# A macaron block on one core: the up product multiplied on GpSimd, the first FFN an item ahead, ten steps for eleven

## What is computed

```python
x = x + 0.5 * ffn(layernorm(x))
x = x + mamba_and_mlp(layernorm(x))
x = x + 0.5 * ffn(layernorm(x))        # the same ffn weights

def ffn(x):                             # mixture of 32 experts of 96, six chosen, and a shared part of 192
    scores = sigmoid(x @ gate_w); combine = top 6 of them, normalised
    act = silu(x @ wg) * (x @ wu)
    return (combine * act) @ wd + (silu(x @ sg) * (x @ su)) @ sd

def mamba_and_mlp(x):
    h = x + mamba(rmsnorm(x))           # projections, conv, softplus, a scan over 256 tokens with 16 states, gate, out
    return h + mlp(rmsnorm(h))          # silu(gate) * up, down, 1024 wide
```

## Time and profile before

| | |
|---|---|
| median of 3 runs | 1908.88 us (1899.79 to 1910.92) |
| the profiled execution | 1911.02 us, its span 1909.2 us |
| mean granted TensorE clock | 0.936 |
| step -1, ends at | 20.7 us |
| step 0 | 93.5 us, to 114.2 |
| step 1 | 180.0 us, to 294.2 |
| step 2 | 200.0 us, to 494.2 |
| step 3, 4, 5, 6 | 217.8, 218.5, 218.4, 218.5 us, to 1367.4 |
| step 7 | 201.9 us, to 1569.3 |
| step 8 | 187.4 us, to 1756.7 |
| step 9 | 85.3 us, to 1842.0 |
| step 10 and the end | 67.2 us, to 1909.2 |

### The profile page before, as it was taken

How to read it: one execution, slowest core, us unless ns; L and a number is a source line. 1 busy time by engine, 2 the same in 40 slices (tenths; PEclk the granted TensorE clock), 3 DMA queues, 4 the chain that set the end, 5 groups by cost and what they waited for, 6 DMA issues and landing times. The chain is left out here.

```text
span 1909.2 us, 25234 instructions
## 1 busy us (share of the span) xinstructions
PE 1600.1 (84%) x7512; PEld 1197.6 (63%) x7512; DVE 1318.9 (69%) x2331; ACT 703.8 (37%) x1418; POOL 724.8 (38%) x838
## 2 busy tenths in 40 slices
PE   6776778667889888889889898888989998677999
PEld 5665557556765557555665557555666566556998
DVE  3236984689468964899468874799559974896343
ACT  4234424533343423534344333534344324532211
POOL 4511552245225532355225532355225632353222
PEclk9887889888899999999999999999999999988999
DMA  7852223323232222322232222222232222323563
GB/s 256 300 165 95 83 93 92 115 83 106 69 107 85 82 79 79 106 75 88 81 101 89 71 85 87 96 79 88 84 97 94 82 90 69 125 94 103 176 211 132
DMA packets 72751, 204.77 MB, mean 107 GB/s; under 512 B 12928, under 2 KB 22368, under 8 KB 72224
## 3 DMA queue, kind: packets, MB, share of 16 engines
q1 hardware_dynamic: 64416, 177.86, 27.9%
q0 software_dynamic: 8192, 25.17, 4.5%
HBM read 179.39 MB, written 15.73 MB: 102 GB/s over the span
## 5 line engine op out<-in xcount | busy, mean ns | idle before, releaser
L610 PE MATMUL gub<-x_hi,wr 128*128 128x256 f32 (+1 forms) x1144 | 454.9, 398 | 76.6 <-DVE hid L978 55.2
L690 PE MATMUL acc<-hid,w_down 128*128 128x256 f32 (+1 forms) x1144 | 419.4, 494 | 0.8 <-DVE hid L978 0.8
L1236 POOL TENSOR_TENSOR hid<-hid,weight 128x256 f32<-128x256 f32 (+1 forms) x264 | 266.6, 1010 | 384.0 <-DVE hid L978 366.6
L612 PE MATMUL gub<-x_hi,wr 128*128 128x256 f32 (+1 forms) x1144 | 394.5, 345 | 0.0
L611 PE MATMUL gub<-x_lo,wr 128*128 128x256 f32 (+1 forms) x1144 | 394.4, 345 | 0.0
L839 ACT ACTIVATE hid<-gub 128x256 f32<-128x256 f32 (+1 forms) x350 | 160.8, 460 | 619.3 <-PE gub L612 530.7
L1249 POOL TENSOR_TENSOR ring<-ring 128x512 f32<-128x512 f32 x192 | 246.7, 1285 | 318.6 <-DVE ring L1133 318.6
L1127 DVE TENSOR_TENSOR_SCAN ring<-decays,side 128x512 f32<-128x512 f32 x256 | 310.2, 1212 | 10.7 <-ACT decays L936 8.3
L610 PEld LDWEIGHTS gub<-x_hi,wr 128*128 128x128 f32 x1144 | 230.1, 201 | 114.3 <-issue 67.9
L690 PEld LDWEIGHTS acc<-hid,w_down 128*128 128x128 f32 x1144 | 212.2, 201 | 86.2 <-issue 67.2
L612 PEld LDWEIGHTS gub<-x_hi,wr 128*128 128x128 f32 x1144 | 229.5, 201 | 23.1
(11 more groups left out here) (115 smaller groups left out, 1691.2 us busy)
## 6 DMA issues: line engine op xcount, KB each, us to landing
wr<-w_halves SPq DMA_DIRECT2D x260, 512.0 KB, 3.3
wm_gu<-in_w_mlp POOLq DMA_DIRECT2D x64, 256.0 KB, 3.0
w_halves<-wr SPq DMA_DIRECT2D x26, 512.0 KB, 4.8
wm_down<-in_w_mlp POOLq DMA_DIRECT2D x64, 128.0 KB, 2.5
w_raw<-in_w_gu SPq DMA_DIRECT2D x26, 256.0 KB, 4.9
cst<-decays SPq DMA_DIRECT2D x192, 32.0 KB, 1.9
...
```

Of the source, the lines that this page charges most:

```text
L610: mm(out, w[:, 0, half, k, :], x_hi[:, k, a:b], start=(k == 0), stop=False)
L612: last = mm(out, w[:, 1, half, k, :], x_hi[:, k, a:b], start=False, stop=(k == KC - 1))
L690: last = mm(acc[k][:, a:b], w, h[:, a:b], start=(c == 0), stop=(c == (MLP_CHUNKS if mlp else FFN_CHUNKS) - 1))
L1236: nc.gpsimd.tensor_tensor(h, h, weight[c // 3 % CSLOTS][:, a:b], ALU.mult).then_inc(sem["weighted"], 1)
```

## The change

Two edits. First, item `u` gets a part on ScalarE, which copies the bank to one of three new SBUF buffers `u_sb` and so frees the bank; `by_u` moves from DVE to POOL, which multiplies `hid` by that buffer, and the subtraction in `ws` moves from POOL to DVE. The MLP's products stay on DVE under a semaphore of their own, `m_hidden`.

Second, the first FFN runs an item ahead. Step 0 has item 0 alone, and norms and routes items 1 and 2. Step 1 takes items 1 and 2 in one 512-wide pass (`twin`); step t from 2 to 6 takes item t+1. The result is kept in `x1_next` and copied over to `x1` by a DMA (`shift`) once mamba has done with that, and the raw x of the next item is then loaded to `x1_next` (`again_n`). The second FFN takes item t-3 in steps 3 to 7 as before; from step 7 on it also takes the item whose MLP ran in the same step (`own`: item 5 in step 7, 6 in step 8, 7 in step 9), in columns 0 to 255. In these steps the MLP, norm `ln2a` and routing are merged with mamba's norms and projections, and the whole FFN pass comes after, merged with the scan. The steps are -1 to 9, the loop has three turns (3, 4, 5). The widths are 256 in steps 0, 2, 8, 9 and 512 in 1 and 3 to 7.

The core of the diff:

```diff
 def items_of(t):
-    first, mamba, mlp, second = (0 <= t - lag < BATCH for lag in range(4))
-    following = t + 1 < BATCH
     if t < 0:
-        return [("load",)] + norm("ln1") + routing("f1")
-    hand = ([("hx", "f1")] if first else []) + ([("hx", "f2")] if second else [])
-    hand += ([("rt2", "f1")] if first else []) + ([("rt2", "f2")] if second else [])
+        return [("load", 0)] + norm("ln1") + routing("f1")
+    mamba, mlp = 0 <= t - 1 < BATCH, 0 <= t - 2 < BATCH
+    first, twin, second, own = t < BATCH - 1, t == 1, 3 <= t < BATCH, t >= BATCH - 1
+    ready = (["f1"] if first else []) + (["f2"] if twin or second else [])
+    hand = [("hx", call) for call in ready] + [("rt2", call) for call in ready]
+    following = t == 0 or t + 2 < BATCH
     keep = [("keep",)] if second else []
-    keep += [("load",)] if following else []
+    keep += [("load", 0)] if following else []
     norms = norm("lnA") + norm("rms1") if mamba else []
     project = ([("split", 0), ("x", 0), ("split", 1), ("x", 1), ("z", 0), ("split", 2), ("z", 1),
                 ("dt", 0), ("dt", 1), ("sp",), ("sp_dt",), ("sp_x",), ("y0",)] if mamba else [])
     units = [(k, u) for u in range(UNITS) for k in ("ub", "unit")] if mamba else []
     last = [("yz",), ("outp",)] + norm("rms2") if mamba else []
-    r0 = ([("r0",)] if mamba else []) + ([("again",)] if first else [])
-    ln2 = norm("ln2") + routing("f2") if mlp else []
+    r0 = [("r0",)] if mamba else []
+    r0 += [("again",)] if t < 2 else [("shift",)] if t < BATCH else []
+    r0 += [("again_n",)] if 1 <= t < BATCH - 1 else []
+    ln2 = norm("ln2") + routing("f2") if mlp and not own else []
     ln1 = norm("ln1") + routing("f1") if following else []
+    if t == 0:
+        ln1 = ln1[:1] + [("load", 1)] + ln1[1:] + norm("ln1b") + routing("f2")
     ahead = [(k, c) for c in range(MSLOTS) for k in ("mgn", "mdn")] if 0 <= t + 1 - 2 < BATCH else []
-    ff = ffn_items(t, first, second)
+    ff = ffn_items(t)
     along = norms + project
-    length = LENGTH if first and second else SHORT
+    length = LENGTH if twin or first and second else SHORT
     scan = r0 + (merge(units, ln2 + ln1, length) if units else ln2 + ln1) + last
     if not mlp:
         return hand + keep + merge(ff[:-TAIL], along + scan, length) + ahead + ff[-TAIL:]
-    if not mamba:
-        return hand + keep + mlp_items() + ahead + merge(ff[:-TAIL], scan, length) + ff[-TAIL:]
+    if own:
+        chain = mlp_items() + ahead + norm("ln2a") + routing("f1") + [("rt2", "f1"), ("hx", "f1")]
+        if not mamba:
+            return chain + ff
+        return hand + keep + merge(chain, along, LENGTH) + merge(ff[:-TAIL], scan, LENGTH) + ff[-TAIL:]
     heavy = mlp_items() + ahead + ff
     return hand + heavy[:6] + keep + merge(heavy[6:-TAIL], along + scan, length) + heavy[-TAIL:]
...
-def ffn_items(t, first, second):
-    if not (first or second):
-        return []
-    splits, more = t == 0, t + 1 < BATCH + 3
+def ffn_items(t):
+    splits, more = t == 0, t + 1 < BATCH + 2
...
-    return out + ([("end", "f1")] if first else []) + ([("end", "f2"), ("store",)] if second else [])
+    if t < BATCH - 1:
+        out += [("end", "f1" if t < 2 else "f1n")]
+    if t == 1:
+        out += [("end", "f1b")]
+    if 3 <= t < BATCH:
+        out += [("end", "f2"), ("store",)]
+    return out + ([("end", "f2a"), ("store_own",)] if t >= BATCH - 1 else [])
...
-    "gub": {"g": [("gated", 1)], "u": [("hidden", 1)], "gum": [("hidden", 1)]},
+    "gub": {"g": [("gated", 1)], "u": [("u_copied", 1)], "gum": [("m_hidden", 1)]},
...
+                if it[0] == "shift":
+                    sp.wait_ge(sem["r_base"], s.count("r_base", ("r0",), 1))
+                    sp.dma_start(x1[:], x1_next[:]).then_inc(sem["shifted"], 16)
+                if it[0] == "again_n":
+                    if ("shift",) in s.at:
+                        sp.wait_ge(sem["shifted"], s.count("shifted", ("shift",), 16))
+                    sp.dma_start(x1_next[:], d["x"][s.t() + 1]).then_inc(sem["x_again_n"], 16)
...
+                elif kind == "u":
+                    c = it[2]
+                    a, b = spans[s.n]
+                    act.wait_ge(sem["u_filled"], s.count("u_filled", it, 1))
+                    if c >= USLOTS:
+                        act.wait_ge(sem["hidden"], s.count("hidden", ("by_u", "ff", c - USLOTS), 1))
+                    elif (least := s.prior("hidden")) is not None:
+                        act.wait_ge(sem["hidden"], least)
+                    A(u_sb[c % USLOTS][:, a:b], s.gub_of(it)[:, a:b], ACT.Copy).then_inc(sem["u_copied"], 1)
...
-                elif kind in ("by_g", "by_u"):
+                    v.tensor_tensor(h, h, b[:, SEQ:2 * SEQ], ALU.mult).then_inc(sem["m_hidden"], 1)
+                elif kind == "by_g":
                     c = it[2]
                     a, b = spans[s.n]
                     h = hid[c % HSLOTS][:, a:b]
-                    if kind == "by_g":
-                        of = ("g", "ff", c)
-                        dve.wait_ge(sem["tanh_done"], s.count("tanh_done", of, 1))
-                        v.scalar_tensor_tensor(h, h, 1.0, s.gub_of(of)[:, a:b], ALU.add,
-                                               ALU.mult).then_inc(sem["gated"], 1)
-                    else:
-                        of = ("u", "ff", c)
-                        dve.wait_ge(sem["gated"], s.count("gated", ("by_g", "ff", c), 1))
-                        dve.wait_ge(sem["u_filled"], s.count("u_filled", of, 1))
-                        v.tensor_tensor(h, h, s.gub_of(of)[:, a:b], ALU.mult).then_inc(sem["hidden"], 1)
+                    of = ("g", "ff", c)
+                    dve.wait_ge(sem["tanh_done"], s.count("tanh_done", of, 1))
+                    v.scalar_tensor_tensor(h, h, 1.0, s.gub_of(of)[:, a:b], ALU.add,
+                                           ALU.mult).then_inc(sem["gated"], 1)
+                elif kind == "ws":
+                    w = wr[it[1] % WSLOTS]
+                    dve.wait_ge(sem["w_hi"], s.count("w_hi", it, 1))
+                    v.tensor_tensor(w[:, 1], w_raw[it[1] % RAWS][:], w[:, 0].bitcast(F32),
+                                    ALU.subtract).then_inc(sem["w_split"], 1)
...
+                    a = SEQ if call in ("f1b", "f2") else 0
                     src, dst, scale = {"f1": (x1, x1, 0.25), "mlp": (res, x2, 0.5),
-                                       "f2": (x2kept, x2kept, 0.25)}[call]
+                                       "f1b": (x1_next, x1_next, 0.25), "f1n": (x1_next, x1_next, 0.25),
+                                       "f2a": (x2, x2, 0.25), "f2": (x2kept, x2kept, 0.25)}[call]
...
-                if it[0] == "ws":
-                    w = wr[it[1] % WSLOTS]
-                    pool.wait_ge(sem["w_hi"], s.count("w_hi", it, 1))
-                    nc.gpsimd.tensor_tensor(w[:, 1], w_raw[it[1] % RAWS][:], w[:, 0].bitcast(F32),
-                                            ALU.subtract).then_inc(sem["w_split"], 1)
+                if it[0] == "by_u":
+                    c = it[2]
+                    a, b = spans[s.n]
+                    h = hid[c % HSLOTS][:, a:b]
+                    pool.wait_ge(sem["u_copied"], s.count("u_copied", ("u", "ff", c), 1))
+                    pool.wait_ge(sem["gated"], s.count("gated", ("by_g", "ff", c), 1))
+                    nc.gpsimd.tensor_tensor(h, h, u_sb[c % USLOTS][:, a:b], ALU.mult).then_inc(sem["hidden"], 1)
```

More of the change, by code:

```diff
@@ L65 @@
     "again": {"x_again": 16},
+    "again_n": {"x_again_n": 16},
+    "shift": {"shifted": 16},
     "hx": {"x_hi": 1, "x_split": 1},
@@ L291 @@
              "outp": [("mixed", 2)]},
[L292 removed]
+    "gub": {"g": [("gated", 1)], "u": [("u_copied", 1)], "gum": [("m_hidden", 1)]},
 }
[L295 removed]
+ENDED_BY = {"g": "by_g", "ub": "unit"}
 BANKS = {"side": SIDES, "gub": GUBS}
@@ L335, in macaron_kernel @@
     ALU, ACT, AX = mybir.AluOpType, mybir.ActivationFunctionType, mybir.AxisListType
-    times = [-1, 0, 1, 2, 3] + list(range(BATCH - 1, BATCH + 3))
+    times = [-1, 0, 1, 2, 3] + list(range(BATCH - 2, BATCH + 2))
     steps = [items_of(t) for t in times]
     LOOP = times.index(3)
-    TURNS = BATCH - 1 - 3
-    spans = [(0 if t < BATCH else SEQ, 2 * SEQ if t >= 3 else SEQ) for t in times]
+    TURNS = BATCH - 2 - 3
+    spans = [(0, 2 * SEQ if t == 1 or 3 <= t < BATCH else SEQ) for t in times]
     led = Ledger(steps, TURNS, LOOP)
@@ L386, in macaron_kernel @@
         comb = sb("comb", [PARTS * EXPERTS, 2 * SEQ], BF16)
+        u_sb = [sb(f"u_sb{i}", [P, 2 * SEQ]) for i in range(USLOTS)]
         weight = [sb(f"weight{i}", [P, 2 * SEQ]) for i in range(CSLOTS)]
@@ L529, in do @@
                 if it[0] == "load":
-                    if (least := s.prior("centered")) is not None:
+                    if it[1]:
+                        sp.wait_ge(sem["centered"], s.count("centered", ("n1", "ln1"), 1))
+                    elif (least := s.prior("centered")) is not None:
```

(18 more changed lines are left out.)

37 lines of the change are left out of this document (22 added, 15 removed).

## The result

The changed kernel took 1865.11 us in the median of 4 runs (1862.36 to 1867.42), the kernel before 1909.9 (1899.79 to 1911.49) in its 4. The ratio is 0.977, with a 95% interval from 0.9754 to 0.9786. The forecast was 1781 in a range from 1728 to 1850: the kernel is faster, but by 45 us and not by 128. The profiled execution had 1864.78 us, its span 1862.6.

A forecast was written before the change was run, and what follows sets the result against it. DVE was taken to pace the scan, with PE a close second beside 512-wide FFNs. Step times summed to 1781 us, against 1911.0 profiled; of the 128 us gained some 64 were the dropped step, 64 the relief. Range 1728 to 1850.

The forecast's parts named there:

- the scan of step 8: Scan beside a 256-column FFN: 95.9 us less moved multiplications and routing, plus more `by_g`, 85, taken as 88.
- Step 9: Last step: MLP 20.9 us, bare norm and routing 16.8, split 1.5, last FFN 65.3; together 105 (bounds 100 and 112).
- rival 5: Slower: POOL becomes the bound through its order, read-out waits staying on top of new work; 2009 us, chance 0.03.
- 110 us for 120.2, a gain of 10.4 per full step: Scan stretch of steps with 512-wide FFN: moving the up multiplication off DVE shortens it so (bounds 0 and 20).
- My own sign of being wrong: Stated beforehand: step 3, forecast at 208 us, taking above 215 would prove the prediction wrong.
- Rival 1: Scan: the relief does not come, PE's 108.57 us with its start-stop pattern keeps the pace; 1836 us, chance 0.17.
- 3 us per step for the routing in the scan: Scan: DVE's small routing operations wait for POOL, whose share rises from 52% to 80%; 3 us more.
- rival 2: Projections: DVE and POOL shut each other out, 24 us over six steps; 1805 us, chance 0.08.
- the front of 60 us in steps 7 and 8: MLP, second norm and routing beside projections, before the FFN: 60 us, between 52 and 72, in step 7.
- rival 4: Dear handovers: fronts of steps 7 and 8 at 75 and 80, step 9's chain 25, step 1 190; 1834 us, chance 0.08.
- 9 us of relief: Step 1: taken off 181.3 us for DVE's lost multiplication, within its forecast of 180 (bounds 168 and 195).
- 8 back: Step 1: 8 us added because its projections lose the MLP that partly covered them; alone they took 64.0 us.

The follow-up runs named there:

- e1_step_only: The changed kernel with its first edit undone (DVE multiplies by the up product from PSUM, weight split on POOL), ten steps kept: 1871.64 us, ratio 0.9816.
- e2_relief_only: The kernel before with only the first edit (ScalarE copies u, POOL multiplies, weight split on DVE), eleven steps: 1914.4 us, ratio 1.0025.
- e5_by_u_narrow: The changed kernel with only POOL's multiplication by the up product done on one column, the rest of that product left out: 1837.18 us, ratio 0.9626.
- e7_drive_narrow: The changed kernel with DVE's first operation in each scan unit (times dtx) done on one column, the rest left out: 1789.95 us in a single run.

## Why the prediction was wrong

**What held.** DVE is the pace where it is truly full: the scan of step 8 was forecast at 88 and took 88.1, though the sum had given 85 and I had added 3 for idle time. Step 9, with its bare chain of norm and routing, came at 101.5 for 105. Step 0 was 96.8 for 93.5, and the durations taken over were nearly right: 1297 and 768 ns for the product on POOL, 594 for the copy, but 788 and not 692 for the split of the weights on DVE. Exposed ScalarE copies or a POOL bound in order (rival 5) were not seen; POOL's waits for read-outs in the scan of step 4 shrank from 39.5 and 11.0 us to 22.1 and 10.8. The copy `shift` cost nothing that shows: steps 3 to 5 of `e1_step_only` took 217.6, 217.3 and 215.1 us.

**The step that failed most** is "110 us for 120.2, a gain of 10.4 per full step". I had taken DVE's busy share of 92% for being the bound, and the time of `by_u` in the stretch for time on the path. The scans of steps 3 to 5 took 119.1, 120.8 and 119.0 us. `e2_relief_only`, `e5_by_u_narrow` and `e7_drive_narrow` show that in them the pace is a chain from side bank to DVE and back, that some of DVE's work fills its gaps, and that work on the chain counts by two thirds and `by_u` by under a third. That was worth 29 us in the scans of steps 3 to 5, 5 in step 2 and 7 in step 6. My own sign of being wrong, step 3 above 215 us, came with 217.3, and PE was busy 90% of the scan of step 4, not 95. Rival 1, to which I gave 0.17, came true in these scans, but not with its 1836 us, and PE's busy 109 us were the bound only in step 7.

**The second** is what POOL gives back, sized at 3 us per step for the routing in the scan. Measured, it is 28 us over the kernel, and its place is fronts and tails. My rival 2, DVE and POOL shutting each other out in the projections, had a real mechanism and a price, 24 us, near the 28; that is partly luck, for the convolutions that it named kept their 476 ns (475 before). In the whole trace none of them met a multiplication on POOL. What met POOL's work were the routing, the start and the gate of y.

**The third** is the front of 60 us in steps 7 and 8. I took FFN chunks out of the queue as if they had been its length. It is a serial chain, and PE waits in it, 13.5 us for the routing alone: 50.28 us busy of 75.5 where I had estimated 43, at a granted clock of 0.80 (rival 4 had 75 and 80). The two fronts cost 29 us more than forecast; step 7's rest was 137 us where I had 142. They are also about what the second edit by itself is short of: it gained 38 us in `e1_step_only`, whose two fronts took 74.3 and 72.3, and not 64.

**The fourth** is step 1: 195.6 for 180. Without the relief it took 196.2 (`e1_step_only`), so the 9 us of relief in its sum did not come, and the "8 back" for its projections was some 7 too little: wide chunks in the front made it 72.6 us for 64.0, and the tail 25.4 for 20.6.

**Open.** Why the wide scan stands at 119 to 121 us with PE at 109 and DVE at 101 is explained only in part: `cmb` in a side bank is 4 us of it, the first operation of the units up to 11, and norms and routing are the likely rest, as PE's idle time of 11, 5 and 0 us with two, one and none of them in the scan suggests. What sets the fronts of steps 3 to 6 was not found; the convolution does not. How the 28 us divide into longer DVE operations, queue order and clock was not separated.
